# Next image's Haar transform during the last head, a second bank for the first maxima, and a new order between images

## What is computed

```python
ll = (x1 + x2 + x3 + x4) * 0.5                     # x1..x4: the four pixels of a 2x2 block
high = concatenate([lh, hl, hh], axis=1)
attn = einsum('bhnd,bhmd->bhnm', l2norm(q), l2norm(k)) * scale
_, idx = top_k(attn, 512)                          # rest set to -1e9
out = einsum('bhnm,bhmd->bhnd', softmax(attn), v)
ll_out = group_norm(conv1x1(out, proj_w), g, b, 32)
y = silu(group_norm(depthwise3x3(high, dw_w), ...))
high_out = high + alpha * group_norm(conv1x1(y, pw_w), ...)
out = x + 0.1 * iwt(ll + ll_out, high_out)
out = out + 0.1 * group_norm(conv1x1(gelu(group_norm(conv1x1(out, w1))), w2))
# layer 1
attn = softmax(einsum('bnr,brm->bnm', q, k) * scale)   # 4096 x 4096, r = 16
out = gamma * (Wo @ (v @ attn.T) + bo) + x
```

## Time and profile before

| | us |
|---|---|
| median of 3 runs | 6230.21 |
| profiled execution, its own time | 6232.92 |
| its span | 6231.1 |
| PE busy (matmul) | 4863.4 (78%) |
| DVE busy | 4701.6 (75%) |
| ACT busy | 4546.7 (73%) |
| POOL busy | 401.7 (6%) |

### The profile page before, as it was taken

How to read it: one execution, slowest core, us unless ns; L and a number is a source line. 1 busy time by engine, 2 the same in 40 slices (tenths; PEclk the granted TensorE clock), 3 DMA queues, 4 the chain that set the end, 5 groups by cost and what they waited for, 6 DMA issues and landing times.

```text
span 6231.1 us, 91139 instructions
## 1 busy us (share of the span) xinstructions
PE 4863.4 (78%) x30180; PEld 3035.4 (49%) x30180; DVE 4701.6 (75%) x8351; ACT 4546.7 (73%) x6907; POOL 401.7 (6%) x133
## 2 busy tenths in 40 slices
PE   4343778886888868887888868887888868885888
PEld 2000345653556435653656535563556535562566
DVE  3676689976899678976889769886898769984443
ACT  3886579956998479956999479976899569983223
POOL 3000300011000300011000300002000200000000
PEclk7555789987999879997999879997899979997999
DMA  1001200012000110012000120012000120011000
GB/s 62 7 9 38 75 9 18 12 53 67 16 16 35 60 39 16 14 55 67 14 16 12 57 63 18 16 54 68 9 18 14 51 69 14 18 36 37 9 11 9
DMA packets 104798, 199.90 MB, mean 32 GB/s; under 512 B 36632, under 2 KB 41656, under 8 KB 100184
## 3 DMA queue, kind: packets, MB, share of 16 engines
q1 hardware_dynamic: 104280, 193.56, 10.1%
HBM read 110.61 MB, written 82.05 MB: 31 GB/s over the span
## 4 chain that ended last, share of the span: by engine, by line
DVE 30%; issue 23%; PE 18%; ACT 18%; POOL 5%; DMA 3%; SPq 1%; DVEq 0%; ACTq 0%; POOLq 0%
ACT work L923 11%; DVE MX L1482 9%; PE PS L527 6%; DVE M L1333 5%; DVE arena L1411 5%; PE PS L493 4%; ACT work L941 3%; DVE work L1325 3%; POOL RN L2012 3%; DVE work L1293 3%; DVE work L1317 2%; ACT work L948 2%; PE PS L465 2%; PE PS L436 1%; ACT arena L913 1%
## 5 line engine op out<-in xcount | busy, mean ns | idle before, releaser
L923 ACT ACTIVATE work<-arena,T 128x1024 bf16<-128x1024 f32 x1792 | 2039.6, 1140 | 90.8 <-DVE T L1280 61.5
L527 PEld LDWEIGHTS PS<-V,work 128*128 128x128 f32 x16384 | 2016.7, 195 | 119.7 <-ACT work L948 29.2
L527 PE MATMUL PS<-V,work 128*128 128x129 f32 x16384 | 2046.0, 279 | 22.4 <-ACT work L948 22.4
L1482 DVE TENSOR_REDUCE MX<-PS 128x1 f32<-128x512 f32 x2048 | 1408.2, 688 | 548.7 <-PE PS L493 539.4
L948 ACT ACTIVATE work<-PS 128x1024 f32<-128x1024 f32 x1024 | 1039.6, 1015 | 414.8 <-PE PS L511 414.7
L493 PE MATMUL PS<-KP,QP 96*128 96x512 bf16 x2048 | 853.1, 417 | 464.4 <-DVE MX L1482 435.0
L1411 DVE SCALAR_TENSOR_TENSOR arena<-PS,work 128x1024 f32<-128x1024 f32 x512 | 625.0, 1221 | 192.8 <-ACT work L941 192.8
L493 PEld LDWEIGHTS PS<-KP,QP 96*128 96x128 bf16 x2048 | 201.0, 98 | 1037.6 <-DVE MX L1482 960.7
L511 PE MATMUL PS<-QP,KP 99*128 99x512 bf16 x2048 | 621.8, 385 | 70.8 <-ACT work L948 39.1
L913 ACT ACTIVATE arena<-PS 128x1024 f32<-128x1024 f32 x512 | 520.9, 1017 | 162.8 <-PE PS L436 161.7
L1333 DVE MAX8 M<-work 128x8 f32<-128x1024 f32 x512 | 625.6, 1222 | 3.0
(11 more groups left out here) (180 smaller groups left out, 3968.3 us busy)
## 6 DMA issues: line engine op xcount, KB each, us to landing
scr<-work SPq DMA_DIRECT2D x96, 256.0 KB
work<-scr SPq DMA_DIRECT2D x128, 192.0 KB, 2.7
work<-in_x SPq DMA_DIRECT2D x16, 1024.0 KB, 5.2
arena<-in_x SPq DMA_DIRECT2D x8, 2048.0 KB, 11.0
scrX<-arena SPq DMA_DIRECT2D x8, 2048.0 KB, 14.2
XR<-scrX SPq DMA_DIRECT2D x64, 256.0 KB, 2.7
out<-YO SPq DMA_DIRECT2D x64, 256.0 KB, 2.1
scrL<-work SPq DMA_DIRECT2D x24, 512.0 KB, 15.0
```

What stands on the lines that cost most here:

```text
L527: last = mm(PS[:, 5 + i // 2, 136 * (i % 2):136 * (i % 2) + 129], P1[:, (16 * j + k) % 3, t, 128 * i:128 * i + 128], V1[:, mt, :], start=( ...
L923: A(JKA[:, m % 2, :], scores(h, i), ACT.Sign, scale=-1.0, bias=T[:, h % 2, i:i + 1], accum_out=CA[:, h % 2, i:i + 1]).then_inc(s["ca"], 1)
L1482: V.reduce_max(MX[:, c % 2, i, w:w + 1], PS[:, 4, :], AX.X).then_inc(s["mr"], 1)
```

## The change

1. JA moves to two new units of `work` (12, 13), which grows from 12 to 14. The exponentials no longer share Xin's place.
2. SP loads the first half of the next image at the start of head 7's second half of work (after `dls`), no longer after the last mask. POOL's `pairs` wait for the counts of head 7 (`ca`, `cd`), and `bands(0)` for the transposed scores of head 6 instead of `oc`. OC and OB move to units 5 and 6 of `arena`; their first load waits for `xg` (the last `base`).
3. Head 7's `weigh` 3 to 7 go between the slot's `score_t` and layer 1 steps, the last one ahead of `l1_weigh(7, 15)`.
4. The maxima of chunk 0 alternate between banks 4 and 6, and PE waits for the reduce before the last one.
5. `between` has a new order on PE, ACT, DVE and POOL, with waits adapted to it.

```diff
-        work = sb("work", [128, 12, N0])
+        work = sb("work", [128, 14, N0])
-        JA, JD = work[:, 0:2, :], work[:, 2:4, :]
+        JA, JD = work[:, 12:14, :], work[:, 2:4, :]
-        OC, OB = places(11, 1), places(9, 1)
+        OC, OB = units(5, 1), units(6, 1)
+        def maxbank(c, k):
+            return 6 if c == 0 and k % 2 else 4
...
                     if l0 and h == NH - 1:
                         load_parts(b)
+                        if more:
+                            sp.wait_ge(s["dls"], (b + 1) * 48)
+                            sp.sem_inc(s["free"], 1)
+                            load_x(b + 1, 0)
...
                     if l0 and h == NH - 1:
+                        sp.wait_ge(s["xg"], (b + 1) * 4)
+                        sp.sem_inc(s["free"], 1)
                         load_done(b, True)
-                        if more:
-                            sp.wait_ge(s["p"], (b + 1) * (NH * NT))
-                            sp.sem_inc(s["free"], 1)
-                            load_x(b + 1, 0)
...
-                    pe.wait_ge(s["mr"], a * 256 + c * 32 + k + 1)
+                    pe.wait_ge(s["mr"], a * 256 + c * 32 + k + (0 if c == 0 and k else 1))
+                    if c == 0 and k == 1 and l0:
+                        pe.wait_ge(s["de"], (b + 1) * 6)
-                    mm(PS[:, 4, :], QP1[0:KS, c * 512 + 128 * i:c * 512 + 128 * i + 128], KP1[0:KS, 512 * w:512 * w + 512],
+                    mm(PS[:, maxbank(c, k), :], QP1[0:KS, c * 512 + 128 * i:c * 512 + 128 * i + 128], KP1[0:KS, 512 * w:512 * w + 512],
+                def last_weigh(h, i):
+                    if h == NH:
+                        weigh(h - 1, i)
                     score_t(h - 1, 5)
+                    last_weigh(h, 3)
                     l1_score(h - 1, 13)
...
                     maxrow(h)
+                    last_weigh(h, 7)
                     l1_weigh(h - 1, 15)
...
                     if k == 0:
                         pool.wait_ge(s["xin"], (n + 1) * 32)
+                        if fin:
+                            pool.wait_ge(s["ca"], (f + 1) * ACT_ALL)
+                            pool.wait_ge(s["cd"], (f + 1) * DVE_ALL)
...
-                            pool.wait_ge(s["oc"], f + 1)
+                            pool.wait_ge(s["st"], (f * NH + NH - 1) * NT)
...
-                power(f, n, fin, opn, 3)
                 norms()
-                power(f, n, fin, opn, 1)
                 repeat()
+                power(f, n, fin, opn, 3)
+                power(f, n, fin, opn, 1)
```

More of the change, by code:

```diff
@@ L634, in slots @@
                     maxrow(h)
+                    last_weigh(h, 7)
                     l1_weigh(h - 1, 15)
-                    weigh(h - 1, 3)
-                    weigh(h - 1, 4)
-                    weigh(h - 1, 5)
+                    for i in range(3, 6):
+                        if h < NH:
+                            weigh(h - 1, i)
                     score(h + 1, 0)
@@ L812, in between @@
                 conv(0, 0, 1)
+                values0(0)
                 qk0(1)
+                proj(0)
+                proj(1)
+                qk0(2)
+                group(0)
+                qk0(3)
+                ungroup(0)
                 conv(0, 0, 2)
-                qk0(2)
+                squares()
+                conv(0, 1, 0)
                 ffn1(0)
@@ L832, in between @@
                 ffn1(15)
-                squares()
+                conv(0, 1, 1)
                 group(3)
-                conv(0, 1, 0)
+                values0(1)
                 ungroup(3)
-                conv(0, 1, 1)
+                spread(0)
                 conv(0, 1, 2)
+                spread(1)
                 ffn2(0)
@@ L1182, in between @@
                 gelu(3)
+                ffn2(0)
                 gelu(4)
                 gelu(5)
-                ffn2(0)
-                conv(0, 0)
+                part0(0, 0)
+                ffn2(1)
+                conv(0, 1)
                 gelu(6)
+                ffn2(2)
                 gelu(7)
-                ffn2(1)
-                ffn2(2)
                 ffn2(3)
-                conv(0, 1)
                 ffn2(4)
@@ L1819, in points @@
                         mark["bh"] = ch.n
+                taps(2, 0)
+                taps(2, 1)
+                taps(1, 0)
+                taps(2, 2)
                 heads_out()
+                taps(1, 1)
                 proj(0)
@@ L1825, in between @@
                 variance(0)
+                taps(2, 3)
                 scales(0)
+                taps(1, 2)
                 add0(0)
@@ L1855, in between @@
                 moments(3)
[L1856 removed]
                 variance(3)
[L1858 to L1859 removed]
+                taps(2, 5)
+                taps(1, 6)
                 scales(3)
[L1861 to L1864 removed]
+                taps(2, 6)
+                normal(0)
+                taps(2, 7)
                 taps(1, 7)
+                conv(0, 1)
                 taps(1, 8)
[L1867 to L1870 removed]
                 conv(1, 0)
                 conv(1, 1)
+                taps(2, 8)
+                normal(1)
                 conv(2, 0)
+                ffn2(0)
                 conv(2, 1)
+                ffn2(1)
                 moments(1)
                 variance(1)
[L1877 to L1880 removed]
                 ffn2(2)
```

139 lines of the change are left out of this document (58 added, 81 removed).

## The result

The changed kernel takes 6086.98 us (median of 4 runs, 6078.1 to 6091.87) against 6230.99 for the kernel before in the same comparison. The ratio is 0.977, 95% interval 0.975 to 0.979: 2.3% faster, 144 us. The forecast was 6061 with a range of 6020 to 6112, so the gain came out 25 us smaller than forecast. The profiled execution (6086.94 us) shows that the forecast was right for reasons that partly cancel.

The account below looks back on a forecast made before the run. No engine was the bound; waits in the boundary and chunk 0's maxima were. Maxima -94, boundaries -84, first boundary -3, image 0 +10 and +2 gave -169 us: 6061 from 6230.2, range 6020 to 6112.

Parts of the forecast that it names:

- Two banks: Chunk 0's maxima: two products in flight give 0.61 to 0.70 us a reduce instead of 1.39; 94 us in sum.
- 0 to 10 are paced by ACT's counts, so both stay: In `first()`, maxima 0 to 10 and 11 to 14 keep their pace; only the 15 from k = 15 gain, 10.4 us.
- Head 7, its sums and the transform: Boundary up to the end of `heads_out`: POOL's pairs delay DVE's `base` and `mix`, early weighs cost PE; +4.0 us.
- heads_out to ffn1(0): Boundary's opening: faster projections, no small DVE stalls, a shorter gap after the last `add0`; 15.5 us instead of 22.15, -6.7.
- PE has no qk0(2) left, only a conv: Before ffn1(0), the gap after the last `add0` shrinks from 3.2 to 1.2 us, -2.0.
- ffn1(0) to Gelu: Boundary: fewer products and taps save 5 us, norm 3's power behind the long one costs 4.6; -0.9 with the rest.
- Gelu to qk1: Boundary: PE's own work of 39.7 us plus 0.8 for waits replaces 48.9; -8.4 us, if no engine's order blocks another.
- qk1 to the maxima: After qk1 nothing changes: score and DMA chain follow as before, and SP's stores of the parts start 14 us earlier.
- Image 0: First image: norm 1 some 20 us later behind power and repeat, query parts and first score 10 us later; +10 us.
- the boundary's order gains little: Rival: the boundary's new order brings only -4 us an image, 6117 us in all; chance 0.17.
- a clock that stays up: Rival: PE's clock rises during the nearly continuous maxima; with `base` also unblocked, 6020 us; chance 0.15.
- The late clamp: Slower rival: a clamp late in the boundary delays everything; at 2109 no gain, at 2114 about 6265 us; chance 0.03.

Follow-up runs that it names:

- the written-out kernel: The changed kernel with its loop over images 1 to 6 written out on all five engines, order kept: 6035.97 us.

## Why the prediction was right, and where it was not

That the sum lies within 25 us is in part luck: the second bank brought 106 to 113 us where 94 were forecast, all the rest 25 to 39 where 75 were. By its own signs the prediction stands on the edge. The period of this image shrank by 17.8 us, inside the 15 to 30 that it set, but qk1 came 5.9 us earlier, just under the 6 below which it called itself wrong.

**Two banks: right, undersized.** The mechanism was right to the row: 0.696 us a reduce. The sum had 94 us, measured were 106 to 113. The term "0 to 10 are paced by ACT's counts, so both stay" is what was small. In the changed kernel DVE takes the first three without a pause:

```profile
2160.03 2.09 DVE L1498 TENSOR_REDUCE MX<-PS 128x1 f32<-128x512 f32 x3 [0.90 <-PE PS L500]
```

At one bank that group took 3.5 us. From the first reduce to DVE's first own count it was 15.4 us and is 13.0. In the mean of the seven boundaries, 11.8 us an image were gained on the kernel before and 13.2 on the changed kernel, not 10.4.

**Head 7, its sums and the transform: right in sum.** `base` was held by POOL like a tensor_tensor (3.32 and 2.64 us against 1.22). The prediction took it as the same because its two inputs are the same; the trace agrees beside POOL's pairs, but beside its long power a tap with two SBUF inputs kept its 1.27 us. The masks, which read PSUM, took 1.17 to 1.23 us beside POOL. Of the 3.4 us by which the last mask came later, the lock is 2.8. The prediction saw that `l1_weigh(15)` would stand behind `weigh(7)`, but not that before it ran while DVE was still at the last mask. That put `head_out` 2.6 us later, and hid inside the +4.2, because I had not asked what it would be without.

**heads_out to ffn1(0): the step that failed.** Forecast -6.7, measured -1.4 here and -1.8 behind the loop. The step let `proj` start when `heads_out` ends and let PE do the rest at its good speed. Where both held, behind image 6 in the written-out kernel, it came out: 16.0 us from the end of `heads_out` to ffn1(0), 15.5 forecast. So miscounting PE's line is not what broke it, although "PE has no qk0(2) left, only a conv" counted one convolution where two stand behind `ungroup(0)`, with the squares between: that line took 9.4 us there. In the boundary of the rows the stretch took 20.8 us. `proj`, itself at its good speed (1.88 us, as forecast), started 3.6 us behind `heads_out`, because the first convolution had lost 2.8 us to a pause at the loop's end and 1.8 us to its own slowness; and the last convolution ahead of ffn1(0) took 4.30 us for 2.82. Behind the loop there was no pause, but PE's line took 14.0 us at a clock of 0.71 to 0.76. I had given neither the loop's end nor a fall of the clock in the opening a term. In the kernel before, the loop's end lay behind the transfer of OC and the next image's pixels, and writing it out there shortened the five boundaries by 7.7 us; in the changed kernel it shortened them by 28. At the lower clock the three steps of that stretch took 4.6 us more behind image 6 (14.0 for 9.4) and 4.8 more behind image 0. The clamp, which hangs on the same line, came 63.4 us behind the store where the forecast had 59.0 (2086.5 on the scale of the rows).

**ffn1(0) to Gelu: right in kind, -0.2 for -0.9.** Norm 3's power waited behind `repeat` as foretold, from 2083.42, when its input was there, to 2086.34. The repeat lasted 2.54 us and the power 1.51, where I had 2.0 and 0.6.

**Gelu to qk1: held.** -8.7 us against -8.4, called the least sure term. It is PE's own work, as in the sum: from 2090.71 to qk1 PE has no wait that the timeline lists.

**qk1 to the maxima: 1.3 us longer**, where I had 0. SP's stores of layer 1's parts start 1.6 us after their input, behind the loads of the heads on SP's queue, and at once before. The stores of the next image's parts, which I had 14 us earlier, came 4.9 us earlier (118.2 us behind head 7's store for 123.1).

**Image 0: +13.5 us for +10**, by the mechanism given. Putting norm 1 ahead of the spreads took it all back.

**The rivals.** The one that came true in part is the first, that the boundary's order gains little: it had -4 us an image, and in the loop all but the bank brought 3.1 to 5.5. Its 6117 was missed because the second bank brought more than forecast. The rival with a clock that stays up was refuted in the maxima (0.50 throughout) and matters in the opening, where I had not looked for it. In the opening and behind norm 3 the granted clock came down: it was 0.50 behind the 3.05 us without `conv(0, 0, 2)`, and 0.66 around the 4.12 us behind norm 3 in the boundary of the rows. The late clamp never came near 2109: it was 63.4 us behind the store, 82.6 before.

**Open.** What the 2.8 us at the loop's end are made of, the jump or the fetching of instructions behind it, no run here separates. Nor is it known why the clock fell in one execution and not in another with the same pauses.

## What to carry to other kernels

When a change removes the wait that ends a stage, list what that wait had covered on each engine, a loop's end among them, and price it before summing the gain. Work on PE that fills a wait can be cheaper in place than out of it: moving two convolutions out of the way made the kernel 19 us slower. And undo each part of a change alone: here one of them seems to have worked against the rest, by some 13 us in its one run.

## What the runs showed of the hardware

- In the changed kernel the loop's end, in front of work that nothing else delayed, showed as 2.5 to 2.9 us of "issue" on PE and 1.7 to 1.8 us on DVE, and the first three products behind it took 4.2 to 5.4 us. With the loop written out there was no such pause, and they took 2.74.
- Without `conv(0, 0, 2)`, a pause of PE of 3.05 us was followed by a granted clock of 0.50 and squares of 7.00 us; behind a pause of 0.28 us they took 3.74 us in the changed kernel, and 3.74 to 5.34 with its loop written out. Behind image 6, the clock of the same stretch was 0.71 to 0.76 in the first and 1.00 in the second, and ffn1(0) came 4.4 us earlier in the second.
- In the changed kernel a scalar_tensor_tensor with two SBUF inputs (`base`) was held until POOL's streaming instruction ended, and itself ended 1.1 us behind it (3.32 us for 1.22); the masks, with a PSUM input, took 1.17 to 1.23 us beside the same pairs. POOL's pairs took 2.83, 3.68, 3.80 and 2.84 us beside DVE's `base`, `mix` and masks, and 2.82 to 2.84 beside masks alone.
- Not every POOL instruction held DVE. During the power of 21.70 us a tap, with two SBUF inputs, took its 1.27 us; beside the repeat (2.54 us) two of them took 4.10:

```profile
2069.02 1.27 DVE L1808 SCALAR_TENSOR_TENSOR work<-PAD,w_dw,work 128x1024 f32<-128x1024 f32 x1
...
2083.35 4.10 DVE L1808 SCALAR_TENSOR_TENSOR work<-PAD,w_dw,work 128x1024 f32<-128x1024 f32 x2
```
